# Two heads per product with V, and four kinds of steps in self attention

## The chip, the cores and the metric

One core of a Trainium2 chip runs the kernel. The metric is the time of one execution in device microseconds, the median of 3 runs.

## The reference

x is (8, 512, 512): eight batches of 512 rows. A cross attention with a context of 77 rows a batch and one key of the row itself, then self attention in 16 heads of 32 and a mixture of eight experts, of which each row takes two:

```
x = x + xattn(layernorm(x), ctx)
    # scores: [q.k_own, q.k_ext] -> softmax -> p[0] * v_own + p[1:] @ v_ext
x = x + ffn(layernorm(x))
    # q, k, v = split(h @ W_qkv + b_qkv), 16 heads of 32
    # attn = softmax(q @ k.T / sqrt(32)) @ v
    # gate = softmax(h @ W_gate + b_gate); top 2 of 8 experts
    # ffn = attn + sum over the two of gate * (h @ W_e + b_e)
```

## The kernel before

Every fp32 product with weights is made of three fp32r products (`prod3`, L219 to L223): high by high, high by low and low by high part. ACT writes the high part of each operand, DVE subtracts it and writes the low part.

**Tiles of cross attention.** 32 tiles of 128 rows run through a software pipeline, `steps` in each engine's block. In a step, ACT's list of work is p_hi of the tile before (L700), weigh (L705, the exponential of the scores), h_hi (L667), h_norm (L656), h2_hi (L680), gate_out (L688), h2_norm (L656 again, the normalised rows for the next layer, tile before) and chunk_hi (L694). The last one has nothing to do with the tile: it casts one of 32 chunks (128 x 512) of the experts' weights, whose low half DVE writes (chunk_lo, L1293) and SP stores (L358). SP loads chunk t + 1 (L354) in its iteration t, after the stores of h2 of tile t - 1 (L382, it waits for h2_norm) and of turned h2 (L347), and after the store of chunk t - 1 (L358). Chunks have two buffers. PE's step is score (L921 to L926: the product with the keys, `s_keys`, then with A, `s_full`), extend, h_turn, gate, value and p_turn. DVE's `largest` (L1255 to L1264) reads `s_keys` first, then `s_full`, and ends with the maximum for which weigh waits.

**Batches of self attention.** 16 steps a batch, one head (k) each; eight batches, six of them in a loop. The order on PE, ACT and DVE is written by hand in `STEP`, with two kinds of step. The tokens:

- S0 to S3: scores of head k, 128 queries by 512 keys each (PE, L1037), into one bank each; m0 to m3: their row maximum (DVE, L1528); E0 to E3: exponential in place, which gives only the row sums (ACT, L762). S of a head waits for E of the head before in the same bank. The suffix @1 or @2 means the head one or two steps before.
- s: the maxima split in two parts (DVE); n: they are turned into a row (PE, L1046) in bank 6, and DVE puts them into the stack of operands (L1542).
- T0, T2: the scores again, turned, with the maximum subtracted by the product itself, two chunks of keys each (PE, L1057); t0, t2: their exponential, the probabilities PT (ACT, L772). PT has four buffers, one a head.
- PV: four heads' product with V (PE, L1073; plain fp32, each matmul leaves two records), 32 output partitions a head, so four heads fill the four column groups; it is done in two runs, a (key chunks 0, 1) and b (2, 3). ACT copies the result (L777), OT turns it back (PE, L1084) and DVE scales it into tmp (`finish`, L1550 to L1556); bank 6 serves PV, OT and n.
- D: the next item of the projections. Items R0 to R3 are queries and keys of the batch's second half of heads, N0 to N3 of the next batch's first half, V0 to V3 its values. Each is 12 matmuls of 512 columns into bank 2, in two halves Da and Db; then ACT writes the high part (L719) and DVE the low (L1313), or DVE adds the bias for V (L1308).

`PLAN` gives the items and groups to the steps: a PV step is k = 1, 5, 9, 13, each other step has an item. SP copies the projections into stacks (L411), fetches the turned rows of the next batch once R3 is made (`fetch_turned`, L351, four transfers of 512 KB, into the buffer that R3 has read), and POOL adds tmp to the output in DRAM every 8 heads (`attended`, L544) and scatters the routing's records (L562).

## Time and profile before

| | us |
|---|---|
| median of 3 runs (1448.44 to 1458.95) | 1453.66 |
| the profiled execution | 1453.07 |
| its span | 1451.4 |
| PE busy | 1325.3 (91%) |
| DVE busy | 947.3 (65%) |
| ACT busy | 910.6 (63%) |
| POOL busy | 361.2 (25%) |

From the page's slices, each 36 us, with busy tenths and the clock that PE was granted:

```profile
PE   4989999999799899999999999999998879999987
PEld 4967888888666566656666566665665347777775
DVE  4256788878768878777777777777777623433332
ACT  4123444444338789989899898998999833333332
```

Slices 4 to 11 are the tiles, 13 to 32 the batches, the rest the expert blocks. A busy PE is not PE at its peak, since matmuls overlap; a wait stands in brackets behind a row.

### The profile page before, as it was taken

The page shows a single profiled execution, that of the slowest core. Times are in us where ns is not written, and L with a number is a line of the kernel's source. Part 1 is how long each engine was busy: PE and PEld are TensorE (multiplying, and loading weights), DVE is VectorE, ACT ScalarE, POOL GpSimd, SP SyncE. Part 2 cuts the span into 40 slices and gives each one's busy share as a digit, 9 for nine tenths or more (in the row PEclk, how much of TensorE's full clock was granted, in tenths as well). Part 3 has the DMA queues.
Part 4 walks back from the last instruction along what each step waited for, and adds up shares of the span by engine and source line. Part 5 has one row for each costly group of instructions (what it writes and reads, how often), then busy time and mean ns, then how long its engine had stood idle before and what let it go on. Part 6 is the DMA issues. An engine that isn't in the chain of part 4 may idle for free.

```text
span 1451.4 us, 25227 instructions
## 1 busy us (share of the span) xinstructions
PE 1325.3 (91%) x6720; PEld 969.9 (67%) x6721; DVE 947.3 (65%) x2047; ACT 910.6 (63%) x1856; POOL 361.2 (25%) x572
## 2 busy tenths in 40 slices
PE   4989999999799899999999999999998879999987
PEld 4967888888666566656666566665665347777775
DVE  4256788878768878777777777777777623433332
ACT  4123444444338789989899898998999833333332
POOL 0001222222200011210212102120001017777765
PEclk9999999999899999999999999999998779999998
DMA  5005677666664237444464444644449668877873
GB/s 159 1 23 203 244 250 246 244 231 250 211 192 132 51 97 160 95 118 103 105 159 92 119 101 107 159 90 121 101 107 268 233 204 147 144 130 127 144 134 53
DMA packets 111369, 212.44 MB, mean 146 GB/s; under 512 B 28266, under 2 KB 36586, under 8 KB 109140
## 3 DMA queue, kind: packets, MB, share of 16 engines
q1 hardware_dynamic: 82048, 166.13, 38.4%
q0 software_dynamic: 26624, 42.04, 17.3%
q10 hardware_dynamic: 2643, 3.65, 0.8%
q8 instruction: 24, 0.39, 0.1%
q14 instruction: 30, 0.24, 0.1%
HBM read 79.48 MB, written 77.73 MB: 108 GB/s over the span
## 4 chain that ended last, share of the span: by engine, by line
PE 56%; DVE 14%; issue 9%; ACT 8%; DMA 8%; POOL 3%; POOLq 1%; ACTq 0%; DVEq 0%; SPq 0%
PE banks L221 10%; PE banks L223 10%; PE banks L222 10%; PE banks L1073 8%; PE banks L1057 7%; PE banks L1037 7%; DMA out_dram<-plain,score_bias 4%; ACT plain L772 3%; DVE st L1222 3%; ACT banks L762 2%; DMA plain<-h_rows,score_bias 2%; DVE plain L1528 1%; DVE plain L1270 1%; DVE plain L1259 1%; PE banks L1130 1%
## 5 line engine op out<-in xcount | busy, mean ns | idle before, releaser
L221 PE MATMUL banks<-parts 128*128 128x512 f32 (+6 forms) x1108 | 435.4, 393 | 23.6 <-issue 6.6
L223 PE MATMUL banks<-parts 128*128 128x512 f32 (+6 forms) x1108 | 422.1, 381 | 0.0
L222 PE MATMUL banks<-parts 128*128 128x512 f32 (+6 forms) x1108 | 421.8, 381 | 0.0
L1528 DVE TENSOR_REDUCE plain<-banks 128x1 f32<-128x512 f32 x512 | 329.1, 685 | 75.6 <-PE banks L1037 66.0
L762 ACT ACTIVATE banks<-banks,plain 128x512 f32<-128x512 f32 x512 | 339.2, 664 | 25.2 <-DVE plain L1528 23.1
L772 ACT ACTIVATE plain<-banks 128x1024 f32<-128x1024 f32 x256 | 263.0, 1027 | 45.7 <-PE banks L1057 43.9
L221 PEld LDWEIGHTS banks<-parts 128*128 128x128 f32 (+1 forms) x1108 | 213.5, 193 | 66.8 <-issue 33.2
L223 PEld LDWEIGHTS banks<-parts 128*128 128x128 f32 (+1 forms) x1108 | 212.6, 192 | 39.5
L222 PEld LDWEIGHTS banks<-parts 128*128 128x128 f32 (+1 forms) x1108 | 213.7, 193 | 34.1
L1037 PE MATMUL banks<-parts 96*128 96x512 f32 x512 | 207.5, 443 | 23.0 <-ACT banks L762 22.3
L1057 PE MATMUL banks<-parts 104*128 104x512 f32 x512 | 174.6, 423 | 10.3 <-ACT plain L772 10.1
L1037 PEld LDWEIGHTS banks<-parts 96*128 96x128 f32 x512 | 95.8, 193 | 114.4 <-ACT banks L762 81.9
L544 POOL DMA_DIRECT2D out_dram<-plain x16 | 22.2, 1390 | 597.9 <-DVE plain L1556 515.3
L815 ACT CAST parts<-banks 128x512 fp32r<-128x512 f32 x72 | 42.2, 588 | 172.0 <-PE banks L1130 133.3
L1073 PE MATMUL banks<-plain,parts 128*32 128x512 f32 x1024 | 127.9, 619 | 14.8 <-ACT plain L772 14.0
L1606 DVE TENSOR_TENSOR plain<-banks,plain 128x512 f32<-128x512 f32 x72 | 49.8, 692 | 137.4 <-PE banks L223 116.1
L597 POOL DMA_INDIRECT out_dram<-plain,score_bias x72 | 114.1, 1584 | 51.9 <-issue 27.2
L1057 PEld LDWEIGHTS banks<-parts 104*128 104x128 f32 x512 | 94.3, 197 | 43.5 <-ACT plain L772 23.3
L1542 DVE TENSOR_TENSOR parts<-banks,plain 8x512 fp32r<-8x512 f32 x128 | 89.2, 697 | 48.1 <-PE banks L1046 31.6
L762 ACT ACTIVATION_READ_ACCUMULATOR banks<-banks,plain 128x1 f32 x512 | 105.9, 207 | 0.0
L705 ACT ACTIVATE sc<-sc,col 128x78 f32<-128x78 f32 x32 | 11.6, 363 | 129.2 <-DVE col L1264 129.2
L512 POOL TENSOR_TENSOR mo<-mo,consts 128x1 f32<-128x1 f32 x64 | 12.3, 192 | 315.6 <-DVE mo L1226 315.6
(180 smaller groups left out, 1495.0 us busy)
## 6 DMA issues: line engine op xcount, KB each, us to landing
parts<-parts SPq DMA_DIRECT2D x384, 128.0 KB, 2.5
experts_split<-parts SPq DMA_DIRECT2D x32, 512.0 KB, 4.2
h_turned<-parts SPq DMA_DIRECT2D x32, 512.0 KB, 2.9
parts<-h_turned SPq DMA_DIRECT2D x32, 512.0 KB, 7.1
parts<-experts_split SPq DMA_DIRECT2D x8, 2048.0 KB, 8.6
plain<-in_x_dram SPq DMA_DIRECT2D x32, 256.0 KB, 4.1
plain<-in_L_ffn_W_experts_dram SPq DMA_DIRECT2D x32, 256.0 KB, 4.2
out_dram<-plain SPq DMA_DIRECT2D x32, 256.0 KB, 2.3
```

Of the source, the lines that this page charges most:

```text
L221: pe.matmul(out, stat[0], mov[0], start=first, stop=False)
L222: pe.matmul(out, stat[0], mov[1], start=False, stop=False)
L223: return pe.matmul(out, stat[1], mov[0], start=False, stop=last)
L597: pool.indirect_dma_start(out=out_rows, out_offset=bass.IndirectOffsetOnAxis(ap=lst[:, i, 0:1].bitcast(U32), axis=0), in_=ysb[i % 4], in_o ...
L762: act.activation(bank[SB[t]][:], bank[SB[t]][:], ACT.Exp, bias=nmx[:, k, t:t + 1], accum_out=Z[:, t, k:k + 1]).then_inc(q["f_exp"], 1)
L772: act.activation(PT[k % HG][:, c:c + 2, :], banks[0][:], ACT.Exp).then_inc(q["f_pt"], 1)
L1037: pe.matmul(bank[SB[t]][:], stk[slot][0][0:M0, m, t * P:(t + 1) * P], stk[slot][1][0:M0, m, :], start=True, stop=True).then_inc(q["f_s_ful ...
L1057: pe.matmul(bank[c % 2][:], stk[slot][1][0:M1, m, c * P:(c + 1) * P], stk[slot][0][0:M1, m, :], start=True, stop=True).then_inc(q["f_t_ful ...
L1073: last = pe.matmul(bank[6][at_o * HD:(at_o + 1) * HD, :], V[:, c, head * HD:(head + 1) * HD], PT[i][:, c, :], start=(c == 0), stop=(c == T ...
L1528: dve.tensor_reduce(nmx[:, k, t:t + 1], bank[SB[t]][:], AX.X, ALU.max, negate=True).then_inc(q["f_max"], 1)
L1542: dve.tensor_tensor(stk[slot][0][M0:M1, m, :].rearrange("p (t n) -> p t n", t=T), bank[6][M0:M1, 0:P].unsqueeze(1).broadcast_to([2 * T, T, ...
L1606: dve.tensor_tensor(ysb[k % 4], bank[2 + k % 2][:], be_all[:, bass.ds(e * D, D)], ALU.add).then_inc(q["m_sum"], 1)
```

## The change

In the tiles, ACT's chunk_hi moves from the last place of the step to the second, and PE multiplies the first of the four chunks with A ahead of the key products. In the batches, PV is done for two heads at a time: a head's 512 queries go in two halves of 256 columns into two column groups. A batch has eight pairs, in the odd steps, both runs (Pa, Pb) next to each other; copy (o), turning back (O) and finish come eight times with half the size. The items are given to the steps in halves (`HALVES`), by four kinds of step in turn; H is ACT's high part. Step and wait counts follow (NQ = 8 pairs for NG = 4 groups).

```diff
-        PLAN = ["R0", "PV3", "R1", "R2 OT3", "R3", "PV0", "V0", "V1 OT0", "N0", "PV1", "N1", "N2 OT1", "N3", "PV2", "V2", "V3 OT2"]
+        HALVES = (("R0a", "R0b"), ("R1a",), ("R1b", "R2a"), ("R2b",), ("R3a", "R3b"), ("V0a",), ("V0b", "V1a"), ("V1b",),
+                  ("N0a", "N0b"), ("N1a",), ("N1b", "N2a"), ("N2b",), ("N3a", "N3b"), ("V2a",), ("V2b", "V3a"), ("V3b",))
...
+        KINDS = ("whole", "begun", "both", "ended")
         STEP = {
-            "dense": {"pe": "S0 S1 T2@2 n@1 S2 Da S3 OT T0@1 Db",
-                      "act": "E3@1 t2@2 E0 E1 t0@1 D E2",
-                      "dve": "s@1 D@1 m0 n@1 m1 m2 m3 OT"},
-            "PV": {"pe": "T2@2 S0 n@1 S1 S2 PVa S3 T0@1 PVb",
-                   "act": "t2@2 E3@1 E0 E1 t0@1 E2 PV",
-                   "dve": "s@1 n@1 D@1 m0 m1 m2 m3"}}
+            "whole": {"pe": "S0 T2@2 S1 S2 n@1 D0 S3 O T0@1 D1",
+                      "act": "E3@1 t2@2 E0 E1 t0@1 E2 H1",
+                      "dve": "D0@1 s@1 m0 m1 n@1 m2 m3 O"},
+            "begun": {"pe": "n@1 T2@2 S0 S1 S2 Pa Pb T0@1 S3 D0",
+                      "act": "t2@2 E3@1 E0 o t0@1 E1 E2",
+                      "dve": "s@1 n@1 m0 m1 D1@1 m2 m3"},
+            "both": {"pe": "S0 n@1 T2@2 S1 D0 S2 S3 O T0@1 D1",
+                     "act": "E3@1 t2@2 H0 E0 E1 t0@1 E2",
+                     "dve": "s@1 m0 n@1 m1 D0 m2 m3 O"},
+            "ended": {"pe": "S0 T2@2 S1 n@1 D0 S2 S3 T0@1 Pa Pb",
+                      "act": "E3@1 t2@2 E0 H0 E1 t0@1 E2 o",
+                      "dve": "s@1 m0 m1 n@1 m2 m3"}}
...
-                    for d, work in ((-1, p_hi), (0, weigh), (1, h_hi), (2, h_norm), (-2, h2_hi), (-3, gate_out), (-1, h2_norm), (0, chunk_hi)):
+                    for d, work in ((-1, p_hi), (0, chunk_hi), (0, weigh), (1, h_hi), (2, h_norm), (-2, h2_hi), (-3, gate_out), (-1, h2_norm)):
...
-                if c == 0:
-                    await_ge(act, "f_pv", 2 * (b * NG + k // HG) - 1)
-                if c == 2:
-                    await_ge(act, "f_pv", 2 * (b * NG + k // HG))
+                await_ge(act, "f_pv", 2 * (b * NQ + k // 2 - HG // 2) + 1 + c // 2)
                 act.wait_ge(q["f_t_full"], (b * NH + k) * T + c + 2)
...
-                act.copy(Osb, bank[6][:]).then_inc(q["f_o_sb"], 1)
+                act.copy(Osb, bank[6][:, 0:QW]).then_inc(q["f_o_sb"], 1)
...
+                own_key(u, 0)
                 for c in range(C):
                     place = G.rearrange("p b k w -> p (b k w)")
...
-                await_ge(pe, "f_o_sb", b * NG + (k - 1) // HG)
-                await_ge(pe, "f_o_fin", b * NG + (k - 3) // HG)
+                if k % 2:
+                    await_ge(pe, "f_o_sb", b * NQ + (k - 1) // 2)
+                else:
+                    await_ge(pe, "f_o_fin", b * NQ + (k - 2) // 2)
...
                 for c in (0, 1) if half == "a" else (2, 3):
-                    for i in range(HG):
-                        jj, m = i // 2, i % 2
-                        at_o, head = 2 * m + jj, 8 * (g // 2) + HG * m + 2 * (g % 2) + jj
-                        last = pe.matmul(bank[6][at_o * HD:(at_o + 1) * HD, :], V[:, c, head * HD:(head + 1) * HD], PT[i][:, c, :],
-                                         start=(c == 0), stop=(c == T - 1))
+                    for m in range(2):
+                        head = 8 * (p // HG) + HG * m + p % HG
+                        for x in range(2):
+                            o = 2 * m + x
+                            last = pe.matmul(bank[6][o * HD:(o + 1) * HD, 0:QW], V[:, c, head * HD:(head + 1) * HD],
+                                             PT[(2 * p + m) % HG][:, c, x * QW:(x + 1) * QW], start=(c == 0), stop=(c == T - 1))
                 last.then_inc(q["f_pv"], 1)
...
-                for t in range(T):
+                for t in range(T // 2):
                     last = pe.transpose(bank[6][:, t * P:(t + 1) * P], Osb[:, t * P:(t + 1) * P], ident[:])
...
-                if g % 2 == 0:
-                    await_ge(dve, "f_att_out", (2 * b + g // 2) * 16)
+                if p % HG == 0:
+                    await_ge(dve, "f_att_out", (2 * b + p // HG) * 16)
```

How the rows move. In what follows, a line number is the file's own, and the new file's are a few higher: L694, L700, L705, L667 and L656 before are L698, L704, L709, L671 and L660 after. ACT, one step of a tile, before; the chunk's cast (L694) closes the step:

```order
L700 CAST parts<-banks 78x128
L705 ACTIVATE sc,col<-sc,col 128x78
L667 CAST parts<-banks 128x512
L656 ACTIVATE plain<-plain,mo 128x512
L680 CAST parts<-banks 128x512
L688 COPY plain<-banks 16x256
L656 ACTIVATE plain<-plain,mo 128x512
L694 CAST parts<-plain 128x512
```

After, the same step:

```order
L704 CAST parts<-banks 78x128
L698 CAST parts<-plain 128x512
L709 ACTIVATE sc,col<-sc,col 128x78
L671 CAST parts<-banks 128x512
L660 ACTIVATE plain<-plain,mo 128x512
L684 CAST parts<-banks 128x512
L692 COPY plain<-banks 16x256
L660 ACTIVATE plain<-plain,mo 128x512
```

The cast of the chunk now stands between the cast of the turned probabilities and the exponential of the scores.

PE, the step with PV in the loop, before (L1046 is n, L1037 S, L1057 T, L1073 PV; ISA and REGISTER_ALU rows belong to waits):

```order
L1046 MATMUL banks<-ident,neg_max_parts 104x128
L298 REGISTER_ALU
L1037 MATMUL banks<-parts 128x512
L298 REGISTER_ALU
L1037 MATMUL banks<-parts 128x512
L1063 REGISTER_ALU
L1064 REGISTER_ALU
L1073 MATMUL banks<-plain,parts 32x512 x8
L1037 MATMUL banks<-parts 128x512
L1057 MATMUL banks<-parts 128x512 x2
L1073 MATMUL banks<-plain,parts 32x512 x8
```

After, a "begun" step from its third score on (L1083 is PV, L1064 T, L1042 S, L222 to L224 the half item):

```order
L1042 MATMUL banks<-parts 128x512
L1077 ISA
L1083 MATMUL banks<-plain,parts 32x256 x8
L1077 REGISTER_ALU
L1083 MATMUL banks<-plain,parts 32x256 x8
L302 REGISTER_ALU
L1064 MATMUL banks<-parts 128x512 x2
L1042 MATMUL banks<-parts 128x512
L1111 REGISTER_ALU
L992 ISA
L222 MATMUL banks<-parts 128x512
L223 MATMUL banks<-parts 128x512
```

The two runs of PV have come together with half the columns, a step has them every second time, and half an item closes it, V0a in step 5.

## Rows read from the trace of the kernel before

**Rows 1.** Windows, two stretches: PE, PEld, DVE, ACT, POOL busy, clock, DMA share.
```profile
200.00:300.00 100.00, 98.35 (x582) 82.12 (x580) 79.76 (x240) 43.99 (x100) 24.82 (x96) 1.00 0.70 243
700.00:800.00 100.00, 95.11 (x477) 64.72 (x475) 76.99 (x155) 91.32 (x192) 19.20 (x29) 1.00 0.50 115
```
**Rows 2.** Timeline of ACT in a tile: start, us, operation, idle before.
```profile
248.37 0.60 ACT L694 CAST parts<-plain 128x512 fp32r<-128x512 f32 x1
248.88 0.26 ACT L700 CAST parts<-banks 78x128 fp32r<-78x128 f32 x1
253.13 0.36 ACT L705 ACTIVATE sc<-sc,col 128x78 f32<-128x78 f32 x1 [4.00 <-DVE col L1264]
```
**Rows 3.** Waits, 100 to 400 us: in total, times, longest.
```profile
DVE parts L1293 <- ACT parts L694: 48.9, 32, 2.1
```
**Rows 4.** Timeline of SP's issues over two tiles.
```profile
239.90 0.36 SPq L382 DMA_DIRECT2D h_rows<-plain  x1
...
241.86 0.47 SPq L354 DMA_DIRECT2D plain<-in_L_ffn_W_experts_dram  x1
...
248.49 0.35 SPq L382 DMA_DIRECT2D h_rows<-plain  x1
...
250.31 0.56 SPq L354 DMA_DIRECT2D plain<-in_L_ffn_W_experts_dram  x1
...
257.15 0.35 SPq L382 DMA_DIRECT2D h_rows<-plain  x1
```
**Rows 5.** Line L354, 200 to 300 us: the chunk loads' time to landing.
```profile
DMA to landing us min/median/max: 3.6/4.1/4.5
```
**Rows 6.** Timeline of PE in a tile: first matmul of the scores.
```profile
247.01 0.34 PE L922 MATMUL banks<-parts 128*128 x1 [0.19 <-DVE parts L1235]
```
**Rows 7.** Windows around an idle piece of PE, columns as in Rows 1.
```profile
361.70:365.20 3.50, 0.73 (x5) 0.53 (x5) 3.27 (x5) 1.29 (x3) 0.00 (x0) 1.00 1.00 346
365.20:372.00 6.80, 6.80 (x23) 5.47 (x22) 5.29 (x18) 3.30 (x7) 2.05 (x8) 0.50 0.18 68
```
**Rows 8.** Groups by shape, 600 to 1100 us: exponentials in place.
```profile
L762 ACT ACTIVATE banks<-banks,plain 128x512 f32<-128x512 f32 x352 | 233.0, 662 | 5.8 <-DVE plain L1528 3.9
```
**Rows 9.** Timeline of PE over three steps of a batch.
```profile
713.74 0.23 PE L1046 MATMUL banks<-ident,neg_max_parts 128*104 128x128 f32 x1
...
715.62 1.92 PE L1073 MATMUL banks<-plain,parts 128*32 128x512 f32 x16 [0.49 <-ACT plain L772]
717.48 0.50 PE L1037 MATMUL banks<-parts 96*128 96x512 f32 x1
...
721.26 0.22 PE L1046 MATMUL banks<-ident,neg_max_parts 128*104 128x128 f32 x1
...
726.00 0.22 PE L1046 MATMUL banks<-ident,neg_max_parts 128*104 128x128 f32 x1
...
728.62 0.60 PE L1084 MATMUL banks<-ident,plain 128*128 128x128 f32 x4
...
730.68 0.39 PE L223 MATMUL banks<-parts 128*128 128x512 f32 x1
...
731.84 0.22 PE L1046 MATMUL banks<-ident,neg_max_parts 128*104 128x128 f32 x1
```
**Rows 10.** Timeline of ACT and DVE behind the matmul at 730.68.
```profile
731.11 0.69 ACT L719 ACTIVATE parts<-banks,bias_qk_cols 128x512 fp32r<-128x512 f32 x1 [0.29 <-PE banks L223]
...
731.83 0.75 DVE L1313 SCALAR_TENSOR_TENSOR parts<-banks,bias_qk_cols,parts 128x512 fp32r<-128x512 f32 x1 [0.50 <-ACT parts L719]
```
**Rows 11.** Timeline of PE's weight loads in a run of PV.
```profile
715.62 0.16 PEld L1073 LDWEIGHTS banks<-plain,parts 128*32 128x32 f32 x8 [0.80 <-issue]
...
716.07 0.14 PEld L1073 LDWEIGHTS banks<-plain,parts 128*32 128x32 f32 x4 [0.29 <-issue]
```
**Rows 12.** Line L351, fetches of turned rows to landing, 1009:1012, then 827:830.
```profile
DMA to landing us min/median/max: 4.4/6.7/9.0
...
DMA to landing us min/median/max: 5.7/6.7/8.1
```

More of the change, by code:

```diff
@@ L259, in early @@
             return BEFORE.index(item), HIS.index(item) - 4 if item in HIS else None
+        KINDS = ("whole", "begun", "both", "ended")
         STEP = {
[6 rows of a table removed]
[12 rows of a table added]
         def plan(b, k, engine, first, last):
-            work = PLAN[k].split()
-            kind = "PV" if "PV" in work[0] else "dense"
-            for token in STEP[kind][engine].split():
+            for token in STEP[KINDS[k % 4]][engine].split():
                 what, _, lag = token.partition("@")
                 of, head = (b, k - int(lag or 0)) if k >= int(lag or 0) else (b - 1, k - int(lag) + NH)
-                if first and of is not b:
-                    continue
-                if what[0] == "D":
-                    item = [w for w in PLAN[head].split() if w in ITEMS][-1:]
-                    if not item or (last and of is b and item[0][0] in "NV") or (engine == "act" and item[0] not in HIS):
-                        continue
-                    what = item[0] + what[1:]
-                elif what[0:2] in ("OT", "PV"):
-                    g = [w for w in work if w[0:2] == what[0:2]]
-                    if not g or (first and g[0][2] == "3"):
-                        continue
-                    of, head, what = (b - 1 if g[0][2] == "3" else b), int(g[0][2]), g[0][0:2] + what[2:]
-                yield what, of, head
+                if what[0] in "DH":
+                    half = HALVES[head][int(what[1])]
+                    if (last and of is b and half[0] in "NV") or (engine == "act" and half[0] == "V"):
+                        continue
+                    what = half if engine == "pe" else half[0:2]
+                elif what[0] in "PoO":
+                    pair = (k - 3 - (what == "O")) // 2
+                    of, head = (b, pair) if pair >= 0 else (b - 1, pair + NQ)
+                if not first or of is b:
+                    yield what, of, head
         def await_ge(eng, name, value):
@@ L914, in h_turn, with own_key @@
                 last.then_inc(q["h_tr"], 1)
+            def own_key(u, c):
+                return prod3(pe, bank[1][:, c * P:D], at(hT[u % 2], sl, c), at(A, sl, c, slice(c * P, D)), c == 0, c == C - 1)
             def score(i, u, bb):
@@ L926, in score @@
                 last.then_inc(q["s_keys"], 1)
-                for c in range(C):
-                    last = prod3(pe, bank[1][:, c * P:D], at(hT[u % 2], sl, c), at(A, sl, c, slice(c * P, D)), c == 0, c == C - 1)
+                for c in range(1, C):
+                    last = own_key(u, c)
                 last.then_inc(q["s_full"], 1)
@@ L1095, in batch @@
                             max_turn(of, head)
-                        elif what[0:2] == "PV":
-                            pv(of, head, what[2])
-                        elif what == "OT":
+                        elif what[0] == "P":
+                            pv(of, head, what[1])
+                        elif what == "O":
                             o_turn(of, head)
@@ L1570, in batch @@
                             max_in(of, head)
-                        elif what == "OT":
+                        elif what == "O":
                             finish(of, head)
@@ L1588, in _ @@
             max_in(B - 1, NH - 1)
-            finish(B - 1, NG - 1)
+            finish(B - 1, NQ - 2)
+            finish(B - 1, NQ - 1)
             def rows_lo(i, k):
```

60 lines of the change are left out of this document (32 added, 28 removed).

## The prediction

> **What bounds the kernel now.** I read the page's slices first, then busy time by stage, then the timelines of ACT, SP and PE inside one tile and one batch, then the landing times of the transfers. Three stages matter: 32 tiles of cross attention (about 110 to 390 us), eight batches of self attention (430 to 1170 us), and the expert blocks, which the change leaves alone.
>
> Tiles: PE is busy 98.35 of 100 us [rows 1]. A tile takes 8.6 us, the distance of two SP issues to h_rows, (257.15 - 239.90)/2 [rows 4]. PE still loses a little: it starts the scores 0.19 us late for DVE [rows 6], and DVE itself sits 48.9 us in 32 waits, 1.5 us each, for ACT's cast of a weight chunk (L694) [rows 3]. ACT has room: after the cast and the cast of the turned probabilities (L700) it idles 4.00 us until the maximum is there (L705) [rows 2]. What is not visible in busy shares is the chunk's own load: SP issues it at 250.31, after h_rows at 248.49 [rows 4], and it lands 4.1 us (3.6 to 4.5) later [rows 5], at 254.4. The cast that reads it comes at about 257.0 (a tile after 248.37 [rows 2]). So it has 2.6 us of slack, and only because the cast is the last thing of the step.
>
> Batches: 352 exponentials ran in 500 us, 64 a batch, so a batch takes 500/5.5 = 90.9 us and a step (one head) 5.68 [rows 8]. PE is at 95.11 and ACT at 91.32 of 100 us [rows 1]: neither is full. The rows of n (L1046) cut PE's stream into steps [rows 9]: 713.74 to 721.26 holds a PV (7.52), 721.26 to 726.00 is PE alone (4.74: 20 matmuls of 512 columns, 0.23 each, and n), and 726.00 to 731.84 (5.84) is a latency loop: last matmul of the item at 730.68, ACT's high half at 731.11, DVE's low half at 731.83 [rows 9, 10], with ACT's E2 behind the high half and PE's next S2 behind E2. In the PV step PE waits 0.49 for the turned exponentials and the queue behind it is served late.
>
> **The change part by part.**
>
> (1) Chunk cast first (ACT, tiles). It removes DVE's 1.5 us wait [rows 3]. With that alone hT comes earlier and PE's waits go (0.19 recorded before the scores [rows 6], about as much before the product with pT): 0.45 us a tile at most, 13 us in all. But the cast now stands right behind L700 and ahead of L705, and its load has not landed there. Queued behind it on ACT are L705, the high half of hT, the two norms; behind L705 DVE's share, the second statistics, POOL's 1/sigma, and h2_norm, which ends the step. And SP's next load comes after h_rows of just that h2_norm. This closes a loop, all from rows: h_rows to load 250.31 - 248.49 = 1.82 and 241.86 - 239.90 = 1.96, take 1.9 [rows 4]; landing 4.1 [rows 5]; cast to the next ACT instruction 248.88 - 248.37 = 0.51 [rows 2] and some 0.05 for the semaphore; L705 to h_rows 257.15 - 253.13 = 4.02 [rows 2, 4]. Sum 1.9 + 4.1 + 0.56 + 4.02 = 10.6 us a tile, against 8.6. The store of the chunk before, which the cast also waits for, is issued 0.8 us ahead of the load, so it wants nearly the same. Loads 2 to 31 are in the loop: the first some 3 (an estimate, its step has the cast's whole lead to lose), some 27 cost 1.95, and one tile is long anyway, since the weight casts of the last batch stand in it. Bounds: with landings of 3.6 the loop is 10.1 (+43), with 4.5 it is 11.0 (+70). I take **+55 us**. The saving of 13 is gone, since PE is no longer last.
>
> (2) own_key(0) ahead of the key products (PE). The same matmuls in another order; L1255 on DVE gets its input 0.7 us later while DVE is waiting for nothing there. 0; with the loop open it would be at most 0.7 of DVE's slack.
>
> (3) PV for pairs, 256 columns. Before: 4 groups a batch, each two runs of 16 records, four at a time in the four column groups, 512 columns. A run lasts 717.48 - 715.62 = 1.86 us: 4 rounds of 0.43 and 0.12 of leaving [rows 9, 11]. Now: 8 pairs, 32 records in one go, 8 rounds of 256 columns. The records are twice as many (256 a batch) and the columns the same. A round at half the columns is 0.217; the four weight loads of the next round take 0.14 together and start with the round [rows 11], so they still fit under 0.217. A pair: 8 x 0.217 + 0.12 + 0.1 of entering = 1.97. Bounds for a round, since no 32-wide record with 256 columns is in the trace: 0.217 (columns alone) and 0.36 (load and stream one after the other, 0.14 + 0.217). I take the lower end, because rounds of 512 run at 0.43 exactly as columns would, with the loads under them. The upper end costs 64 x 0.14 = 9 us a batch.
>
> The Trainium skill, "TensorE: Matmul & The Clock Gate" (section "Wait — 56ns, not 53.3ns?"), gives about 62 ns of sequencer work per matmul when instructions are not decoded in hardware; by that a round of four would take 0.25 and the batch 2 us more, an estimate. The trace speaks against it: the eight weight loads that open a run are over within 0.16 us [rows 11].
>
> (4) O in halves. Two transposes in place of four, eight times a batch: four show 0.60 with their tail [rows 9], so I take 0.25 a step; PE's sum over a batch is the same. DVE's finish now comes 8 times, about +2 us a batch on an engine with 23 of 100 us free [rows 1]; ACT's copies of O +0.6.
>
> (5) Steps of four kinds. PE's floor: "whole" and "both" 4.74 + 0.25 = 5.0; "begun" and "ended" 4.74 - 6 x 0.23 + 1.97 = 5.33. Four steps 20.7, against 22.7 now. Stalls that I find by walking the orders: in "both" D1 wants the bank that D0 just filled. From 730.68 the high half starts 0.43 later, takes 0.69, the low half 0.75 [rows 9, 10]: free 2.0 us after D0's last matmul, while PE has 1.4 us to do (S2, S3, O, T0). 0.6, in the two of four "both" steps whose first half is a query or key. n stands first in "begun", behind DVE's finish of the step before: 0.1, four times. PV no longer waits for t2, which ACT starts in front of the step, and E2 no longer stands behind a high half that waits for PE. ACT's work (4.6 us a step, 0.58 a high half, 0.3 an O copy) stays at or under PE's in each kind. Batch: 82.7 + 1.2 + 0.4 = 84.3; with 0.5 for what I don't see, 84.8. Six middle batches save 6 x 6.1 = 36.6. The first is held by DVE's routing work: 3. The last has no dense work behind its first steps, ACT and half clock hold it: 1, and the tail has a PV of two heads less: 1.5. **-42 us.**
>
> (6) V0a waits for its tile. V0a moved from the step after the PV step into "begun": PE reaches it 5.33 - 6 x 0.23 = 3.95 behind the last R half, which frees the buffer, and SP issues the fetch some 0.45 (an estimate) behind that half. The least landing, that of the second of four transfers, is 4.4 in a quiet stretch and 5.7 in one crowded by POOL's accumulate and scatters [rows 12]; the first is issued 0.5 ahead of it and lands no later, by my estimate 3.5 and 5. POOL's accumulate also moves one step ahead, so I take the quiet case: nothing. Crowded it costs 1.5 a batch, 10 in all.
>
> Sum on the profiled execution (1453.07, against the median 1453.66): 1453.1 + 55 - 42 = **1466 us**.
>
> **The rivals.**
> - The chunk load keeps ahead of the cast: the order of SP or a slack that I misread keeps the loop open. Then the tiles gain 13 and the batches 42: 1398, faster. Against it stands that SP's load follows h_rows in both kernels [rows 4]. The loop bites as soon as ACT reaches the cast's new place less than 1.9 + 4.1 = 6.0 us behind h_rows, and it does so after some 0.7 (248.88 with its 0.25, less 248.49 [rows 2, 4]). 0.12.
> - The batches gain little: 256-column rounds near 0.3, DVE's finish late for n, or the crowded fetch. With 15 in place of 42: 1493. 0.18.
> - PE's clock falls in the tiles. PE has 8 us of work for a step of 10.6 (8.6 less its waits), and the 2.6 would come nearly in one piece, before the scores. In the trace such a piece (PE busy 0.73 of 3.5 us) was followed by a stretch at 0.50, the lower of the two levels, 1.2 GHz [rows 7]. At half clock PE's work fills the gap and the loop stays the same; if it overflows by 0.7 a tile, 20 more: 1486. The Trainium skill's page "TensorE: Matmul & The Clock Gate" (section "What's actually happening") has the same rule, activity keeps the full clock; the row agrees. 0.12.
> - The batches gain more: PE's floor of 82.7 in each of the six (-49) and some more at both ends, -55 in all: 1453. 0.08.
>
> **How the numbers follow.** The forecast has 0.50, between 1455 and 1478. A measurement tells 1% here, so slower begins at 1468.2 and faster ends at 1439. Slower: 0.19 of the forecast, 0.18, 0.12: 0.49. Faster: the first rival and 0.02 of the last, 0.14. Same: the rest, 0.37. Range 1446 to 1490; it leaves out the first rival and the outer part of the second.
>
> **What would show it.** Tiles: L705 or the chunk cast on ACT waiting for a DMA about 2 us a tile, PE at 75 to 80% in 200 to 300 us, tile step near 10.6. Batches: 8 rounds in 1.8 us, n to n near 5.0, 5.3, 5.6, 5.3, exponentials of a batch in 84 to 85 us, S3 to D1 with 0.6 idle in "both". I am wrong if a tile stays at 8.6 or less, or if a batch takes over 88.

## The result, and the profile after

The changed kernel takes 1503.22 us (1501.44 to 1510.6), the kernel before 1452.66 beside it: a ratio of 1.0354, 95% interval 1.0302 to 1.0406. That is slower, as the likeliest sign said, but far from 1466 and outside the range. The profiled execution has a span of 1501.4.

The page's busy line, PE's busy tenths and granted clock in slices of 37.5 us, and the group of the chunk's cast (its last two figures: idle time of ACT before it, and what ended it). The last line is the clock of the kernel before, in slices of 36.3 us:

```profile
PE 1351.7 (90%) x7744; PEld 1028.0 (68%) x7745; DVE 968.8 (65%) x2143; ACT 902.2 (60%) x1888; POOL 358.6 (24%) x572
PE   4989989898988889999999999999997769999997
PEclk9998887989899999999999999999997779999998
L698 ACT CAST parts<-plain 128x512 fp32r<-128x512 f32 x32 | 19.9, 620 | 181.5 <-DMA plain<-in_L_ffn_W_experts_dram 181.5
PEclk9999999999899999999999999999998779999998
```

Before, the tiles had a 9 in every slice but one, and 1.00 in [rows 1]; now slices 4 to 11 hold five 8s and a 7, and ACT waits 181.5 us for chunk loads. The second weak place is slices 31 to 33, in the last batch, where the kernel before has low figures too.

Cutting both spans at the rows of n (n comes once a step, so 16 of them are a batch; "last" is the 15 steps from the last batch's first n to its last):

| stretch | before | after | difference | forecast |
|---|---|---|---|---|
| start to the first n (tiles) | 433.0 | 489.3 | +56.3 | +55 |
| first batch | 98.9 | 98.3 | -0.6 | -3 |
| six middle batches | 545.4 | 526.7 | -18.7 | -36.6 |
| last batch, 15 steps | 86.5 | 100.5 | +14.0 | -1 |
| behind the last n | 287.7 | 286.6 | -1.1 | -1.5 |
| span | 1451.4 | 1501.4 | +50.0 | +13 |

**Tiles.** The step went from 8.62 to 10.77 us (mean of tiles 3 to 27, from one start of PE's products with the keys to the next; measured at another instruction the means differ by up to 0.1). Windows (busy us of PE, PEld, DVE, ACT, POOL, then clock, DMA share, GB/s), the first answering [rows 1], the next three the last batch, and behind them two stretches of the last batch in the kernel before:

```profile
200.00:300.00 100.00, 90.12 (x478) 75.64 (x476) 65.39 (x192) 36.40 (x83) 18.71 (x73) 0.88 0.55 195
1138.00:1162.00 24.00, 16.52 (x81) 8.54 (x85) 12.82 (x29) 14.31 (x31) 0.00 (x0) 0.65 0.61 156
1162.00:1186.00 24.00, 18.67 (x105) 9.61 (x100) 15.64 (x34) 19.16 (x42) 1.45 (x1) 0.78 0.97 367
1186.00:1210.00 24.00, 19.63 (x90) 10.53 (x82) 14.02 (x30) 17.24 (x40) 0.00 (x0) 0.64 0.31 100
...
1100.00:1124.00 24.00, 20.44 (x82) 10.51 (x84) 16.92 (x34) 21.88 (x47) 2.00 (x2) 0.77 0.99 278
1124.00:1148.00 24.00, 20.61 (x84) 8.77 (x80) 16.65 (x34) 20.42 (x46) 1.45 (x1) 0.78 0.83 292
```

Timeline of ACT over a tile, the counterpart of [rows 2]:

```profile
238.54 0.26 ACT L704 CAST parts<-banks 78x128 fp32r<-78x128 f32 x1 [0.48 <-PE banks L947]
244.19 0.62 ACT L698 CAST parts<-plain 128x512 fp32r<-128x512 f32 x1 [5.39 <-DMA plain<-in_L_ffn_W_experts_dram]
244.72 0.35 ACT L709 ACTIVATE sc<-sc,col 128x78 f32<-128x78 f32 x1
...
254.79 0.62 ACT L698 CAST parts<-plain 128x512 fp32r<-128x512 f32 x1 [5.95 <-DMA plain<-in_L_ffn_W_experts_dram]
```

SP's issues in the same tile, the counterpart of [rows 4], and the loads' time to landing [rows 5]:

```profile
238.08 0.35 SPq L386 DMA_DIRECT2D h_rows<-plain  x1
...
239.90 0.55 SPq L358 DMA_DIRECT2D plain<-in_L_ffn_W_experts_dram  x1
...
248.72 0.36 SPq L386 DMA_DIRECT2D h_rows<-plain  x1
```

```profile
DMA to landing us min/median/max: 3.6/4.3/4.5
```

The loop closes on these rows: h_rows to load 239.90 - 238.08 = 1.82, landing 4.3, to 244.2 where the cast starts (244.19); cast to weigh 0.53; weigh to h_rows 248.72 - 244.72 = 4.00. Sum 10.65. ACT stands 5.39 us in front of the cast, while weigh, which needs nothing from the cast, stands in the queue behind it.

**Batches.** Timeline of PE in a "begun" step of one batch, in the next batch's, and at the long step of the last one:

```profile
785.69 0.31 PE L1053 MATMUL banks<-ident,neg_max_parts 128*104 128x128 f32 x1
...
787.15 1.93 PE L1083 MATMUL banks<-plain,parts 128*32 128x256 f32 x32
...
791.14 0.50 PE L222 MATMUL banks<-parts 128*128 128x512 f32 x1 [1.16 <-DMA parts<-h_turned]
...
879.74 0.80 PE L222 MATMUL banks<-parts 128*128 128x512 f32 x1 [2.82 <-DMA parts<-h_turned]
880.33 0.63 PE L223 MATMUL banks<-parts 128*128 128x512 f32 x1
...
1135.68 0.39 PE L224 MATMUL banks<-parts 128*128 128x512 f32 x1
1142.53 0.43 PE L1053 MATMUL banks<-ident,neg_max_parts 128*104 128x128 f32 x1 [6.46 <-DVE neg_max_parts L1545]
...
1145.14 3.56 PE L1083 MATMUL banks<-plain,parts 128*32 128x256 f32 x32
```

Waits of batches 1 to 6, counted from 0 (587 to 1114 us; total, times, longest), then of the last batch:

```profile
PE banks L222 <- DMA parts<-h_turned: 8.4, 5, 2.8
```

```profile
DVE plain L1567 <- DMA out_dram<-plain: 6.7, 1, 6.7
```

SP's load of expert 0 (2 MB) in the last batch, and time to landing of the two accumulates issued from 1066 to 1135 us, at 1083.8 and 1127.3:

```profile
1120.83 6.16 SPq L435 DMA_DIRECT2D parts<-experts_split  x1
...
DMA to landing us min/median/max: 7.9/11.1/14.3
```

A pair's product with V takes 1.93 us for 32 records of 256 columns, as priced. But V0a waits for its tile in five batches, once 2.82 us, and the matmuls behind that take 0.63 in place of 0.39 (the granted clock is 0.51 from 878.8 to 885.7 us). In the last batch DVE's first finish waits 6.7 us for POOL's accumulate of the batch before, the one that lands after 14.3 us; n and the whole step stand behind it, and PE runs at a low clock from there to the end (0.65 in the first window above).

### The profile page after: what moved, and what is told of

Read it like the earlier page. It is cut to its first block and busy times, and to the rows that moved or that the text cites. A ratio compares the mean times of both kernels' runs of the same rounds, so it can differ in the third digit from the quotient of the medians.

```text
span 1501.4 us, 27639 instructions
## 1 busy us (share of the span) xinstructions
PE 1351.7 (90%) x7744; PEld 1028.0 (68%) x7745; DVE 968.8 (65%) x2143; ACT 902.2 (60%) x1888; POOL 358.6 (24%) x572
## 5 line engine op out<-in xcount | busy, mean ns | idle before, releaser
L222 PE MATMUL banks<-parts 128*128 128x512 f32 (+6 forms) x1108 | 453.8, 410 | 57.4 <-DVE parts L1245 19.6
L224 PE MATMUL banks<-parts 128*128 128x512 f32 (+6 forms) x1108 | 432.0, 390 | 0.0
L223 PE MATMUL banks<-parts 128*128 128x512 f32 (+6 forms) x1108 | 431.7, 390 | 0.0
L1538 DVE TENSOR_REDUCE plain<-banks 128x1 f32<-128x512 f32 x512 | 339.6, 687 | 95.6 <-PE banks L1042 89.6
L222 PEld LDWEIGHTS banks<-parts 128*128 128x128 f32 (+1 forms) x1108 | 220.8, 199 | 114.9 <-issue 46.9
L224 PEld LDWEIGHTS banks<-parts 128*128 128x128 f32 (+1 forms) x1108 | 219.8, 198 | 41.7
L223 PEld LDWEIGHTS banks<-parts 128*128 128x128 f32 (+1 forms) x1108 | 221.4, 200 | 30.6
L1042 PE MATMUL banks<-parts 96*128 96x512 f32 x512 | 186.5, 417 | 0.7 <-ACT banks L766 0.3
L1064 PE MATMUL banks<-parts 104*128 104x512 f32 x512 | 180.7, 435 | 6.0 <-ACT plain L773 4.6
L1083 PE MATMUL banks<-plain,parts 128*32 128x256 f32 x2048 | 132.2, 401 | 0.2 <-ACT plain L773 0.2
L698 ACT CAST parts<-plain 128x512 fp32r<-128x512 f32 x32 | 19.9, 620 | 181.5 <-DMA plain<-in_L_ffn_W_experts_dram 181.5
L1042 PEld LDWEIGHTS banks<-parts 96*128 96x128 f32 x512 | 99.3, 195 | 38.6 <-issue 8.8
L766 ACT ACTIVATION_READ_ACCUMULATOR banks<-banks,plain 128x1 f32 x512 | 115.1, 225 | 0.0
L1064 PEld LDWEIGHTS banks<-parts 104*128 104x128 f32 x512 | 86.6, 196 | 33.2 <-issue 15.0
L1083 PEld LDWEIGHTS banks<-plain,parts 128*32 128x32 f32 x2048 | 62.2, 114 | 63.3 <-issue 32.1
```

The costliest lines, as they stand in the source:

```text
L222: pe.matmul(out, stat[0], mov[0], start=first, stop=False)
L223: pe.matmul(out, stat[0], mov[1], start=False, stop=False)
L224: return pe.matmul(out, stat[1], mov[0], start=False, stop=last)
L766: act.activation(bank[SB[t]][:], bank[SB[t]][:], ACT.Exp, bias=nmx[:, k, t:t + 1], accum_out=Z[:, t, k:k + 1]).then_inc(q["f_exp"], 1)
L1042: pe.matmul(bank[SB[t]][:], stk[slot][0][0:M0, m, t * P:(t + 1) * P], stk[slot][1][0:M0, m, :], start=True, stop=True).then_inc(q["f_s_ful ...
L1064: pe.matmul(bank[c % 2][:], stk[slot][1][0:M1, m, c * P:(c + 1) * P], stk[slot][0][0:M1, m, :], start=True, stop=True).then_inc(q["f_t_ful ...
```

## The experiments

Twelve kernels, each against the kernel before on the same chip. "Tile" and the other columns are cut as in the table above; they come from the one profiled execution of each kernel.

| | us | ratio, 95% interval | tile | first n | six middle | last | behind |
|---|---|---|---|---|---|---|---|
| e1 | 1441.22 | 0.9937 [0.9917, 0.9957] | 8.62 | 433.7 | 522.7 | 99.8 | 282.7 |
| e2 | 1506.79 | 1.041 [1.0374, 1.0447] | 10.78 | 487.8 | 545.5 | 86.3 | 284.4 |
| e3 | 1421.43 | 0.9816 [0.9792, 0.984] | 8.10 | 413.2 | 522.9 | 99.6 | 282.5 |
| e4 | 1450.74 | 1.0009 [0.9995, 1.0023] | 8.62 | 434.8 | 545.4 | 86.4 | 284.1 |
| e5 | 1433.93 | 0.9867 [0.984, 0.9893] | 8.08 | 413.5 | 545.5 | 86.4 | 284.8 |
| e6 | 1416.07 | 0.9751 [0.9714, 0.9789] | 8.11 | 415.6 | 520.9 | 91.3 | 286.8 |
| e7 | 1410.6 | 0.9705 [0.9681, 0.973] | 8.09 | 413.2 | 511.5 | 100.0 | 285.2 |
| e8 | 1415.87 | 0.9741 [0.9711, 0.9771] | 8.09 | 415.4 | 520.5 | 92.1 | 287.4 |
| e9 | 1425.53 | 0.9819 [0.9789, 0.9849] | 8.07 | 415.5 | 523.6 | 100.2 | 283.8 |
| e10 | 1402.18 | 0.9655 [0.9629, 0.9681] | 8.08 | 414.0 | 511.6 | 89.6 | 285.3 |
| e11 | 1408.04 | 0.9686 [0.9663, 0.9709] | 8.09 | 415.8 | 512.1 | 90.9 | 288.3 |
| e12 | 1392.1 | 0.9599 [0.9582, 0.9617] | 8.10 | 416.5 | 511.9 | 79.7 | 284.0 |

The stretch behind the last n lies between 282.5 (e3) and 287.7 (the kernel before) where no edit touches it; I don't read anything from differences of that size there.

### The tiles: is it the cast's place, and is it the load's loop?

**e1_cast_back**: the changed kernel with the cast last again.

```diff
-for d, work in ((-1, p_hi), (0, chunk_hi), (0, weigh), (1, h_hi), (2, h_norm), (-2, h2_hi), (-3, gate_out), (-1, h2_norm)):
+for d, work in ((-1, p_hi), (0, weigh), (1, h_hi), (2, h_norm), (-2, h2_hi), (-3, gate_out), (-1, h2_norm), (0, chunk_hi)):
```

> The changed kernel with one thing undone: ACT's cast of the weight chunk stands last in the tile's step again. Theory (loop of load, cast, exponential of the scores, h2_norm, next load): the first n of self attention moves from 489 back to 433 us, a tile takes 8.6 us, and the whole is 1503 - 56 = 1447 us. Rival (the tiles are long because PE multiplies by A first, or because its clock falls by itself): the tiles stay over 9.5 us and the whole stays over 1480 us.

**e2_cast_only**: the kernel before with the cast second, nothing else.

```diff
-for d, work in ((-1, p_hi), (0, weigh), (1, h_hi), (2, h_norm), (-2, h2_hi), (-3, gate_out), (-1, h2_norm), (0, chunk_hi)):
+for d, work in ((-1, p_hi), (0, chunk_hi), (0, weigh), (1, h_hi), (2, h_norm), (-2, h2_hi), (-3, gate_out), (-1, h2_norm)):
```

> The kernel before with one thing done: the cast of the chunk in second place. Theory of the loop: 1453 + 56 = 1509 us, a tile 10.3 us, ACT waiting for the chunk's load in nearly each tile. Rival (the cast hurts only together with the new order on PE): within 15 us of 1453.

The cast alone makes 54.8 us of the 56.3 (487.8 - 433.0), and without it they are gone (433.7). Its place is the whole loss of the tiles. e2's time is as forecast, its tile is longer (10.78 against 10.3); e1's time is 6 us under its forecast.

**e3_cast_mid**: the changed kernel with the cast just ahead of h2_norm. **e5_before_mid**: the same place in the kernel before.

```diff
-(-3, gate_out), (-1, h2_norm), (0, chunk_hi)):
+(-3, gate_out), (0, chunk_hi), (-1, h2_norm)):
```

> The changed kernel with the cast just ahead of h2_norm, in the time in which ACT waits for POOL. Theory of the loop: the load has landed there (it lands 1.3 us after the exponential of the scores starts, the cast's place is 2.3 us after it or later), so the loop is open, and DVE no longer waits 1.5 us for the cast: a tile takes 8.1 to 8.3 us and the whole is 10 to 15 us under the kernel with the cast last, 1432 to 1440 us. Rival (any earlier place of the cast delays h2_norm and so the loop over SP): 1450 to 1470 us.

> The kernel before with one edit: ACT's chunk cast stands just ahead of h2_norm. Loop theory: the cast still meets its chunk (its load has landed by then) and DVE no longer waits for it at a tile's start, so a tile takes 8.1 us as in e3, not 8.62; first n of self attention near 413, and the batches stay as before (90.9 each in the loop). Time 1430 to 1434. Beside e3 (1421) it gives the worth of the new self attention alone: some 10 us by my reading of the stretches (19 saved in the six middle batches, 14 lost in the last, 5 saved behind it). Rival: the gain of e3's tiles came from the open order of own_key together with the cast; then tiles stay at 8.4 or more and the time is 1442 or more.

Timeline of ACT in a tile of e3 (L684 is h2_hi, L660 h2_norm):

```profile
244.88 0.57 ACT L684 CAST parts<-banks 128x512 fp32r<-128x512 f32 x1
...
245.61 0.61 ACT L698 CAST parts<-plain 128x512 fp32r<-128x512 f32 x1
246.51 0.82 ACT L660 ACTIVATE plain<-plain,mo 128x512 f32<-128x512 f32 x1 [0.29 <-POOL mo L522]
```

The cast lies in time that ACT spent waiting for POOL's statistics, and DVE has its low part's input before the next step begins. PE is busy 100.00 of 100 us at clock 1.00 between 200 and 300 us, a tile takes 8.1, and it does so with the old self attention too (e5, as forecast to 0.1 us). e3 came out 11 us faster than the low end of its forecast. The difference of e3 and e5 is then the worth of the new self attention as written: 0.5 percent by the two ratios, 0.9 by the two times; the spans show -22.6 us in the six middle batches and +13.2 in the last. The rival for e5, a gain that needs the new order of own_key, falls.

**e4_own_key_only**: the kernel before with the first chunk of own_key ahead of the keys.

```diff
+            def own_key(u, c):
...
+                own_key(u, 0)
...
-                for c in range(C):
-                    last = prod3(pe, bank[1][:, c * P:D], at(hT[u % 2], sl, c), at(A, sl, c, slice(c * P, D)), c == 0, c == C - 1)
+                for c in range(1, C):
+                    last = own_key(u, c)
```

> The kernel before with PE multiplying the first chunk by A ahead of the key products, nothing else. My prediction: no difference, 1450 to 1456 us, a tile 8.6 us. Rival (the key products come later, DVE's maximum too): a tile 0.3 to 0.7 us longer, 1462 to 1475 us. A gain of some 0.2 us a tile is possible, if the switch between narrow and wide products costs PE something.

Nothing, as priced.

**e9_load_first**: the cast stays second, but SP's load is taken out of the loop.

```diff
-                    if t or not first:
-                        store_chunk(b + (t - 1) // T, (t - 1) % T)
-                    if t and (more or t < T - 1):
-                        load_chunk(b + (t + 1) // T, (t + 1) % T)
-                    elif not first and t == 0:
-                        load_chunk(b, 1)
...
                     sp.dma_start(out_t[b * T + t], x1[:, t, :]).then_inc(q[f"x1_out{t}"], 16)
+                    store_chunk(b, t)
+                    if more or t < T - 2:
+                        load_chunk(b + (t + 2) // T, (t + 2) % T)
                     sp.wait_ge(q["h2_ready"], b * T + t + 1)
...
-            store_chunk(NE - 1, C - 1)
```

> The changed kernel with one edit on SP: chunk t is stored and chunk t + 2 loaded right behind the store of x1 of tile t, ahead of the wait for h2_norm of that tile; ACT's cast stays in second place. Loop theory: the tile costs 10.77 us only because SP's load stands behind h_norm's end, which stands behind the cast. Now the load is issued some 3 us earlier and does not wait for the ACT step that its cast opens; the cast is 1 to 2 us late for its place but ends before ACT's 4 us wait for the maximum does. A tile takes 8.1 to 8.2 us as in e3, first n of self attention at 413 to 418, time 1421 to 1427. Rival: the second place of the cast itself harms (ACT's weigh behind it, whatever the load does), or there is too little time to land from x1's store on: 9.5 us a tile or more, time 1465 or more.

Waits of e9, 150 to 350 us (24 tiles), and its ACT timeline; line numbers are e9's, where L694 is the cast and L705 weigh:

```profile
ACT sc L705 <- DVE col L1270: 41.3, 24, 2.2
ACT parts L694 <- DMA plain<-in_L_ffn_W_experts_dram: 30.8, 24, 2.9
```

```profile
242.46 0.62 ACT L694 CAST parts<-plain 128x512 fp32r<-128x512 f32 x1 [1.30 <-DMA plain<-in_L_ffn_W_experts_dram]
244.80 0.36 ACT L705 ACTIVATE sc<-sc,col 128x78 f32<-128x78 f32 x1 [1.71 <-DVE col L1270]
```

The norm that the forecast calls h_norm is h2_norm, as in its first sentence. This is the run that separates place from loop. ACT still waits 1.3 us a tile for the load, in every tile, and the tile takes 8.07: the wait ends before the maximum is there (weigh waits 1.71 more), so it costs nothing that shows (8.10 in e3, without the wait). What cost 2.15 us a tile against the kernel before was that the load waited for the step which the cast opens.

### The middle batches: the fetch behind the scatters

**e7_mid_scatter**: e3 with all three sets of POOL's scatters (four each) behind the accumulate of a batch's first half of heads. Otherwise the first set goes ahead of it, which is right after the accumulate of the batch before, and so at the time of the fetch.

```diff
-                place(PER * b - PER + 1)
                 attended(b, 0)
-                for m in range(1, PER):
+                for m in range(PER):
```

> e3 with one edit: POOL's scatters of the routing's records all stand behind the accumulate of the batch's first half of heads, none ahead of it. Theory that the four middle batches that take 87 to 90 us in place of 85.3 lose their time because scatters and accumulate crowd the fetch of the next batch's rows, for which V0a waits on PE: the first transfer lands in 3.4 to 4 us, the wait of V0a goes from 1.2 to 3 us to under 0.5 in every batch, batches 1 to 6 take 85.3 to 86 each, and the time is 1412 to 1416. Rival: the accumulate alone crowds the fetch (it stays where it is): waits of 1 us or more remain and the time is 1419 to 1422.

Waits of PE on a DMA in batches 1 to 6 of e3, and time to landing of the changed kernel's first fetch at 785.92:

```profile
PE banks L222 <- DMA parts<-h_turned: 7.2, 5, 2.5
```

```profile
DMA to landing us min/median/max: 5.2/5.2/5.2
```

and POOL's work ahead of that fetch in the changed kernel:

```profile
776.12 1.39 POOL L548 DMA_DIRECT2D out_dram<-plain  x1 [25.52 <-DVE plain L1567]
...
784.49 0.98 POOL L566 DMA_INDIRECT slot_list<-records  x1 [0.79 <-POOL records L563]
```

In e7 the accumulate is issued at 779.52 and the fetch at 789.36, again 10 us behind it, and no scatter stands between. Landing of the first two of the fetch's transfers:

```profile
DMA to landing us min/median/max: 3.4/3.8/4.2
```

PE's wait on h_turned is not among e7's waits any more, and all six middle batches take 85.2 to 85.3. It was the scatters that crowded the fetch, not the accumulate: the rival falls. The changed kernel has the same comparison in itself. Its sixth middle batch has no scatters, since POOL's loop with them ends one batch earlier; its accumulate is issued at 1041.4 and its fetch at 1051.3, 10 us behind it as in the others. The first transfer's landing:

```profile
DMA to landing us min/median/max: 3.4/3.4/3.4
```

The batch has no wait and takes 85.1. The trace of the kernel before had it too: the quiet landing of [rows 12] (4.4, fetch at 1009.31) has an accumulate only 5 us ahead of it and no scatter beside it, while in the crowded one (5.7) scatters run from 825.10 on.

```profile
1004.37 1.40 POOL L544 DMA_DIRECT2D out_dram<-plain  x1 [28.12 <-DVE plain L1556]
```

In the changed kernel the batches with the wait took 89.2, 87.1, 86.9, 91.4 and 87.0; against 85.3 that is 15.1 us in five.

### The last batch: the accumulate behind 2 MB loads, and the clock

**e6_mid_expert**: e3 with expert 0's load (2 MB) behind the copies of the stacks.

```diff
                     read_list()
-                    load_expert(0)
...
+                    load_expert(0)
                     load_expert(1)
```

> e3 with one edit: SP issues the load of expert 0's weights (2 MB) not at the start of the last batch but right before that of expert 1. Theory that the last batch's long step (10.4 us n to n) is POOL's accumulate crowded by that load: the accumulate lands some 6 to 7 us after its issue and not 14, DVE's first finish of the batch's second half waits under 1 us for it, and the last batch takes 93 to 95 us in place of 99.6. Time 1415 to 1417. Rival: the accumulate is late anyway (the two-step distance); then the wait stays at 5 us or more and the time at 1421. A loss is possible behind the batch, if expert 0's weights now land late: then the part after the last n grows by what is gained.

The step of 9.65 us in e3 (10.43 in the changed kernel) is gone (3.85 there) and the batch takes 8.3 less, 91.3 against a forecast of 93 to 95. The wait that it removes is that of the batch's first finish. The forecast did not see a later wait: the next accumulate, of the batch's first half of heads, is the crowded one now, and DVE's finish waits 2.8 us for it:

```profile
DVE plain L1567 <- DMA out_dram<-plain: 2.8, 1, 2.8
```

**e8_mid_fill**: e3 with 6 matmuls of 512 columns in place of each missing half item of the last batch.

```diff
+                    if last and of is b and half[0] in "NV" and engine == "pe":
+                        yield "F", b, k
+                        continue
...
+            def fill(b, k):
+                h, j, m = k // 8, k % 8 // 2, k % 2
+                slot = stack_use(b, h, j)[0]
+                pe.wait_ge(q["f_d_free"], number(b, "R3")[0] + 1)
+                for c in range(6):
+                    pe.matmul(bank[DENSE][:], stk[slot][0][0:M0, m, 0:P], stk[slot][1][0:M0, m, :], start=True, stop=True)
...
```

> e3 with one edit: in the steps of the last batch that have no projections left PE runs 6 matmuls of 512 columns for each missing half into the projections' bank, with operands that lie ready; nobody reads them, so the output is the reference's. Theory that the last batch is long because PE idles between its steps and its clock falls to half: with the fill the granted clock stays at 1.00 there, the last steps take 5.0 to 5.7 us as in the middle and the last batch 88 to 92 us in place of 99.6 (the wait for the accumulate, up to 6.5, remains). Time 1410 to 1414. Rival: the extra 1.4 to 2.8 us of matmuls a step cost more than the clock gives back (if the clock falls all the same, they take 2.8 to 5.6 us): 1425 or more.

Windows of e3, then of e8, columns as in the windows of the result (busy us of the five engines, clock, DMA share, GB/s):

```profile
1074.00:1098.00 24.00, 18.75 (x104) 9.65 (x104) 15.41 (x35) 19.12 (x43) 0.00 (x0) 0.79 0.82 296
1098.00:1122.00 24.00, 19.22 (x96) 10.03 (x96) 12.81 (x30) 16.56 (x36) 1.45 (x1) 0.64 0.62 205
```

```profile
1074.00:1098.00 24.00, 24.00 (x156) 17.75 (x155) 18.76 (x43) 22.44 (x50) 1.45 (x1) 1.00 0.90 329
1098.00:1122.00 24.00, 22.07 (x140) 15.40 (x139) 15.50 (x34) 18.77 (x42) 0.00 (x0) 0.93 0.57 180
```

With half again as many matmuls PE does more of the useful ones in the same time: ACT, which has the same work in both, is busy 22.44 of 24 against 19.12. The long step of 9.88 us is still in e8, ahead of these windows (1052 to 1062 us). A low clock remains behind waits: 0.66 from 1062 to 1070.4 us, behind that step, and 0.76 from 1108.4 to 1115.6, behind a later wait of PE of 1.93 us.

The last batch loses 7.5 us of its 99.6; both it (92.1) and the time (1415.87) are just above their forecasts.

**e10_combo** has the edits of e6, e7 and e8; **e11_two** those of e6 and e7.

> e3 with the edits of e6, e7 and e8 together: scatters behind the accumulate, expert 0's load later in the last batch, and matmuls in the last batch's steps where no projections are left (nobody reads them). If the three causes are separate: batches 1 to 6 at 85.3 us each as in e7; the last batch without the 10 us step (e6) and at full clock (e8), 86 to 89 us; behind the last n 283 to 287 as before. 410 to 415 to the first n, so 1397 to 1402 us. Rival: expert 0's load, moved, now crowds what follows, or the filled steps wait for the vector engine anyway: last batch 91 or more, time 1404 or more.

> e3 with the edits of e6 and e7, without the filling matmuls: it tells what the fill is worth once the wait for the accumulate is gone. Batches 1 to 6 at 85.3 us, the last batch about 91 as in e6 (its clock still falls to half between the steps), 1402 to 1406 us. Rival: with the long wait gone and the scatters moved the clock holds without the fill, last batch under 88 and no difference from the version with all three.

Both came out above their forecasts, e10 just so (its last batch at 89.6), e11 by 2 us. e11 is 0.3 percent slower by the ratios, whose intervals overlap, and its last batch is only 1.3 us longer; the rest of the difference lies in the tiles, the first batch and behind the last n. So the fill's worth beside the other two edits is not shown here. What held e10 back is one step of 10.93 us, with a wait of DVE's finish of 7.2 us for the accumulate of the first half of heads. Without the fill (e11) the same accumulate is issued at 1084.9, lands after 12.2 us and is waited for 0.6 us.

**e12_hold**: e10, and experts 2 to 7 are loaded only when that accumulate has landed.

```diff
                     load_expert(1)
                     sp.wait_ge(q["f_d_full"], number(b, "R3")[0] + 1)
+                    await_ge(sp, "f_att_out", (2 * b + 1) * 16)
                     load_expert(2)
```

> The version with all three edits of e10, and one more on SP: the loads of experts 2 to 7 wait until the accumulate of the last batch's first half of heads has landed. In e10 that accumulate, issued at 1077.28, landed after 16.0 us, since five loads of 2 MB were issued from 1062.28 to 1066.85, and a step of 10.9 us followed it; in the middle batches it lands in 7.5 to 8.2. Theory: with only two loads ahead of it it lands in some 8 us, DVE's finish and with it n wait for nothing, that step takes 5.7 and the last batch 84 to 86 us in place of 89.6; time 1396 to 1399. Rival: the loads, some 10 us later, are then late for the expert blocks, and the part behind the last n grows by what is gained: 1401 to 1404.

Time to landing of the last two accumulates, of e10 and of e12; the slower of e10's two is the one that DVE waits for, the faster of e12's:

```profile
DMA to landing us min/median/max: 12.2/14.1/16.0
```

```profile
DMA to landing us min/median/max: 5.7/9.2/12.7
```

Windows of e12 over two thirds of the last batch:

```profile
1054.00:1078.00 24.00, 24.00 (x157) 17.79 (x156) 18.41 (x38) 22.38 (x52) 0.00 (x0) 1.00 0.83 263
1078.00:1102.00 24.00, 24.00 (x156) 17.74 (x156) 18.78 (x43) 22.44 (x50) 1.45 (x1) 1.00 0.76 269
```

The step that took 10.93 takes 3.79, the 15 steps 79.7 in place of 89.6 (I had 84 to 86), and nothing is paid behind (284.0). The time is 4 us under the forecast. At 1392.1 us, 4.0 percent under the kernel before, this is the fastest of all versions. No run gives the kernel before the same fill and the same later loads, so how much of the gain needs the new order is open.

## Why the prediction was wrong where it was

(1) **The loop of the chunk load: right.** 10.6 us a tile were forecast and 10.77 measured, +55 and +56.3 to the first n; e2, e1 and e9 show that it is the cast's place through SP's order of issues. The sign was misread: ACT waits 5.4 to 6.0 us for the load and not 2, because its 4 us wait for the maximum [rows 2] is gone into it, and PE was 90% busy and not 75 to 80%, because its clock fell. My upper bound for the term adds up to +68, not +70. The first rival (the loop stays open) is out. One size beside it was off: I bounded what a tile gains from a DVE that doesn't wait for the cast by 0.45 us. e3 and e5 gain 0.52 a tile and about 20 us to the first n, not 13. The pieces that I counted were recorded waits of PE. From 200 to 300 us its records went from 582 to 625 while its busy time only went from 98.35 to 100.00, so most of the gain comes from time that had been counted as busy; which gaps those were no row names.

(2) **own_key(0): right**, by e4.

(3) **PV for pairs: right.** 1.93 us a pair against 1.97 (my terms add up to 1.96), so the round stays near 0.217 and the upper bound (0.36) is out. The Trainium skill, "TensorE: Matmul & The Clock Gate" (section "Wait — 56ns, not 53.3ns?"), has about 62 ns per matmul for instructions that are not decoded in hardware; the 0.25 a round that I estimated from it would make a pair 2.2 us, and no run here shows that.

(4), (5) **Steps of four kinds: right, once nothing crowds them.** 84.8 us a batch were forecast; e7 has 85.2 to 85.3 in each of six, 33.9 us saved against 36.6. The single distances of n that I gave as a sign (5.0, 5.3, 5.6, 5.3) are not there: a quiet batch of e7 has 5.8, 6.3, 5.7 and 3.9, since n stands at another place in each kind of step. Only the sum can be held against my 21.2 for four steps: 85.2 a batch is 21.3. The first batch gained 0.6 and not 3. PE's wait in "both" is there (4.9 us in 12, 0.4 each, 0.8 for its weight loads; I said 0.6).

(6) **V0a's wait: the step that failed first.** I wrote "POOL's accumulate also moves one step ahead, so I take the quiet case: nothing". I had the crowded landing in a row [rows 12] and named accumulate and scatters for it, then let the accumulate's place decide. It was the scatters, which stand right ahead of the fetch (last one at 784.49, fetch at 785.92). The first transfer lands in 5.2, and what this costs is 15.1 us, more than the 10 of my crowded case. The waits themselves are 8.4 of it. Of the rest 5.3 us lie in the two batches with the longest waits (1.9 and 2.8 us), and behind the longer one PE's clock is at 0.51. The batches of 89.2 and 91.4 us are over the 88 that I gave as a sign of being wrong.

**The last batch: the step that failed as well.** I put it at -1: "The last has no dense work behind its first steps, ACT and half clock hold it". Measured +14.0. What I did not price is that the finish comes every two steps, so it wants the accumulate landed two steps after its issue and not four. In the middle batches that is enough (7.4 to 8.1 us to landing), under a load of 2 MB it isn't (14.3). I never walked the wait on f_att_out through the last batch, where other transfers run. e6 shows 8.3 us of the last batch by that load. The other part is the clock: the steps behind run at 0.64 to 0.78, and e8 gets 7.5 back by keeping PE busy alone. The two overlap, since the clock is also low behind the long wait (0.52 from 1142.5 to 1148.7 us). With both away and the later loads held back the new steps take 79.7 (e12), 6.8 less than before; the kernel before had no such help. Its clock in the last batch was low too (0.77 and 0.78 in the windows above); the share that the new order itself adds is not separated.

**The rivals.** "The batches gain little" (1493) named the crowded fetch and came true for the middle, though the batches and the tail together gained 6 us and not its 15. It also named DVE's finish late for n, which is what the last batch has; what made it late there, an accumulate behind a load of 2 MB, it did not name. PE's clock did fall in the tiles (0.88 between 200 and 300 us), and as the rival said itself the gap absorbs it: the loop stays at 10.77. Two separate misses of 18 and 15 us, both from transfers that I had priced as quiet, put the time 13 us above my range. The range took in one such case and not both.

## What to carry to other kernels

Before moving an instruction ahead in an in-order list, ask which transfer it waits for, what issues that transfer, and whether the issuer waits for anything behind the instruction's new place: a loop of that kind makes every step as long as the loop (10.77 us here), while a wait for the same load without the loop (1.3 us a tile, e9) costs nothing. When a buffer's turn is shortened, from four steps to two here, check the landing against the new distance in each stage separately, the first and last passes above all, where bulk loads are under way. When two things crowd a transfer in a row, find another row in which only one of them stands there. And order the bulk behind the small transfer that someone waits for: one wait on SP was worth 8 to 10 us here (e12 beside e10, by ratios and by times).

## What the hardware showed that I had not expected

- Four indirect scatters of 128 records of two words, the last of them issued 1.4 us before a fetch of 512 KB, lengthen the landing of its first transfer from 3.4 to 5.2 us (3.3 to 3.5 in e7's batches 1 to 6, 5.2 to 6.8 in the changed kernel's five with scatters). They are 4 KB together; an accumulate 10 us ahead did no harm.
- The accumulate lands in 7.5 to 8.2 us in quiet batches (e10), in 14.3 with one load of 2 MB issued 6.5 us ahead of it (the changed kernel), in 16.0 with five such loads issued 10 to 15 us ahead (e10), and in 5.7 where no load of 2 MB was under way (e12).
- PE's clock: behind a gap of 6.46 us the same 32 records take 3.56 us where they take 1.93 at full clock, and the granted clock is 0.65 over the 24 us around it. Matmuls whose result nobody reads held it at 1.00 and shortened the batch in e8, in a stretch where PE had been idle 5 of 24 us.
